# Moving GpSimd's scaling of k behind the weight residuals and the decayed q in a linear-attention recurrence

## The chip, the cores and the metric

The kernel runs on one NeuronCore of a Trainium2 chip. The metric is the device time of one execution in microseconds (us). The engines are TensorE (PE; its weight loads are shown as PEld), VectorE (DVE), ScalarE (ACT), GpSimd (POOL) and SyncE (SP, which issues DMAs). Each engine works through its own list in order and waits on semaphores.

## The reference

The input x (4 sequences of 1024 tokens, width 512) is normalised, and goes through a recurrent attention layer with 16 heads of width 128 and through a routed feed-forward layer; their product is added to x. What the change touches is the recurrence:

```python
q = silu(causal_dwconv(xn @ Wq, qconv_w, qconv_b))   # 4 taps
k = silu(causal_dwconv(xn @ Wk, kconv_w, kconv_b))
q = layernorm(q.reshape(Bs, Ls, H, DK), qn_w, qn_b)
k = layernorm(k.reshape(Bs, Ls, H, DK), kn_w, kn_b)
v = (xn @ Wv);  b = sigmoid(xn @ Wb + bb)
def step(S, inp):
    S = (1.0 - b) * S + b * (v_t[..., :, None] * k_t[..., None, :])
    o_t = jnp.einsum('bhvk,bhk->bhv', S, q_t)
```

The affine of a head's k is `k * kn_w + kn_b` behind the normalisation. The feed-forward layer keeps half of the tokens of each sequence by rank of a score.

## The kernel before

The kernel has four stages: the tokens (normalisation, gates, transposes), the recurrence, the feed-forward layer on the kept tokens, and the gated output. The change is in the recurrence, `stage_recurrence`. It treats 64 heads (4 sequences times 16), one head per step i, in a pipeline with lags: in step i the head A = i is projected and convolved, B = i-1 gets its silu, transpose and statistics, C = i-2 is transposed back and made ready, D = i-3 has its updates, scores, states and outputs computed. `nxt` = i+1 is the head whose weights are prepared. Two steps make a pair (par 0 and par 1); the par 1 step also ranks 128 tokens on VectorE, and GpSimd issues a small scatter behind it. Matrices in fp32 are multiplied as high and low parts: ScalarE writes `w_hi`, GpSimd writes the residual `w_lo = w_raw - w_hi`, and the same for `wv_hi`, `wv_lo`, which serve two heads and are made in par 0 steps.

The order of each engine in one step is written out by hand:

- TensorE: project q (L1020 to L1022); turn the normalised q of C, turn q of B (all turns are L999); first half of k's projection; turn k of C; second half; turn k of B; updates of D (L1079); scores of D (L1091); V projection (L1039 to L1041); outputs of D (L1105, L1107). The scores overwrite a half of PSUM from which ScalarE's `tokens(1)` reads: `after_step(pe, "k_tok", B_.i)`.
- ScalarE: silu of q of B (L787); ready(0) of C (L762); tap(0) of A (L772, the convolution's last tap); tokens(0) of B (L782); silu of k; `wv_hi` in par 0 (L803); `w_hi` (L808); ready(1) of C; tokens(1) of B (L782), which copies the turned k into `tok[1]`; tap(1); the normalisation of k in place in `tok[1]` (L821); the output copy of D (L827). tokens(1) has these waits:

```python
if j == 1:
    after_step(act, "k_weighted", B_.i - 1)
```

- VectorE: V times beta (L913); the decay scan of C (L924); ranks in par 1 (L970 to L983); three taps of q of A (L865); statistics of q and k of B (L873); variance (L886 to L894); states of D (L941, L945); scores of D times decays (L950); three taps of k of A (L865); k_state of C times decay (L958); shift (L899) and the normalisation of q (L903).
- GpSimd: `k_weighted` of C (L672, `tok[1]` times the norm's weight into `k_state`); `w_lo` of nxt (L679); `q_cum` of D (L686, q times the running decay); `wv_lo` in par 0 (L693); the add of the affine of C (L697, in place in `k_state`); the power function of B (L702, 1/sqrt of the variance).

TensorE's next step starts with a wait for the three taps of k (`k_conv`) and for `w_hi`, `w_lo`.

Of the kernel before, what the change touches and what calls it, by code (L numbers as in the profile page):

```python
# [7 lines left out]
ALU = mybir.AluOpType  # L8
ACT = mybir.ActivationFunctionType
F32 = mybir.dt.float32  # L10
# [35 lines left out]
def stand(eng, carrier):  # L46


    eng.sem_inc(carrier, 1)
# [414 lines left out]
def stage_recurrence(nc, s, a, scratch, keep, kept):  # L464
# [7 lines left out]
    with ExitStack() as ctx:  # L472
        def sb(name, shape, dt=F32):
            return ctx.enter_context(nc.sbuf_tensor("rc_" + name, shape, dt))

        def two(name, shape, dt=F32):
            return [sb(f"{name}{i}", shape, dt) for i in range(2)]

        def sem(name):
            return ctx.enter_context(nc.semaphore("rc_" + name))  # L480
# [3 lines left out]
        w_raw, w_hi, w_lo = keep["w_raw"], keep["w_hi"], keep["w_lo"]  # L484
        wv_raw, wv_hi, wv_lo = keep["wv_raw"], keep["wv_hi"], keep["wv_lo"]
# [5 lines left out]
        q_cm = two("q_cm", [P, L])  # L491
# [4 lines left out]
        cum_all = two("cum_all", [P, L])  # L496
        dmat = two("dmat", [P, NC, P])
        q_cum = sb("q_cum", [P, L])
# [28 lines left out]
        S = {n: sem(n) for n in names.split()}  # L527
# [6 lines left out]
        cum_loaded = [sem(f"cum_loaded{i}") for i in range(2)]  # L534
# [20 lines left out]
        def after_step(eng, name, i, per=1, part=None):  # L555

            if isinstance(i, int):
                if i < 0:
                    return
                i = min(i, N - 1)  # L560
            eng.wait_ge(S[name], per * i + (per if part is None else part))

        def after_pair(eng, semaphore, pair, per=16):

            if isinstance(pair, int) and pair < 0:
                return
            eng.wait_ge(semaphore, per * pair + per)
# [84 lines left out]
        @block.gpsimd  # L652
        def _(pool):
            nc.gpsimd.memset(minus_half[:], -0.5).then_inc(S["consts_set"], 1)
            for c in range(NC):
                last = nc.gpsimd.tensor_copy(chunk_ident[:, c], ident[:])
            last.then_inc(S["consts_set"], 1)
            nc.gpsimd.iota(token_row[:], pattern=[[1, L]], base=0, channel_multiplier=0,
                           allow_small_or_imprecise_dtypes=True).then_inc(S["consts_set"], 1)
            nc.gpsimd.iota(token_col[:], pattern=[[0, B], [P, NC]], base=0, channel_multiplier=1,  # L660
                           allow_small_or_imprecise_dtypes=True).then_inc(S["consts_set"], 1)
            nc.gpsimd.iota(first_slot[:], pattern=[[L, B], [0, NC]], base=0, channel_multiplier=0,
                           allow_small_or_imprecise_dtypes=True).then_inc(S["consts_set"], 1)

            def step(u, par):
                A_, B_, C_, D_, nxt = (At(u, par, lag) for lag in (0, LAG_B, LAG_C, LAG_D, -1))
                if C_.live:

                    k_tokens = k_state[C_.par]
                    after_step(pool, "k_normed", C_.i)  # L670
                    after_step(pool, "updates_mm", C_.i - 2)
                    nc.gpsimd.tensor_tensor(k_tokens[:], tok[1][:], k_norm_rows[:, 0:1].to_broadcast([P, NC, P]),  # L672
                                            ALU.mult).then_inc(S["k_weighted"], 1)
                if nxt.live:

                    after_step(pool, "w_hi_done", nxt.i)
                    after_step(pool, "k_projected", nxt.i - 2)
                    stand(pool, keep["carrier_pool"])
                    nc.gpsimd.tensor_tensor(w_lo[nxt.par][:], w_raw[nxt.par][:], w_hi[nxt.par][:].bitcast(F32),  # L679
                                            ALU.subtract).then_inc(S["w_lo_done"], 1)  # L680
                if D_.live:

                    after_step(pool, "q_ready", D_.i)
                    after_pair(pool, cum_loaded[D_.par], D_.pair)
                    after_step(pool, "outputs_mm", D_.i - 1)
                    nc.gpsimd.tensor_tensor(q_cum[:], q_cm[D_.par][:], cum_all[D_.par][:], ALU.mult  # L686
                                            ).then_inc(S["q_cum_done"], 1)
                if par == 0 and A_.live and not (isinstance(u, int) and u == 0):

                    after_step(pool, "wv_hi_done", u)  # L690
                    after_step(pool, "v_projected", A_.i - 1)
                    stand(pool, keep["carrier_pool"])
                    nc.gpsimd.tensor_tensor(wv_lo[:], wv_raw[:], wv_hi[:].bitcast(F32), ALU.subtract  # L693
                                            ).then_inc(S["wv_lo_done"], 1)
                if C_.live:
                    after_step(pool, "k_weighted", C_.i)
                    nc.gpsimd.tensor_tensor(k_state[C_.par][:], k_state[C_.par][:],  # L697
                                            k_norm_rows[:, 1:2].to_broadcast([P, NC, P]),
                                            ALU.add).then_inc(S["k_tokens_done"], 1)
                if B_.live:  # L700
                    after_step(pool, "small_done", B_.i, 6)
                    nc.gpsimd.tensor_tensor(small[:, 6], small[:, 5], minus_half[:], ALU.pow  # L702
                                            ).then_inc(S["rstd_done"], 1)

            pool.wait_ge(S["consts_loaded"], 16 * 7)

            def pair_steps(u):
                step(u, 0)
                step(u, 1)
                scatter(u)  # L710

            def scatter(u):

                pool.wait_ge(S["slot_done"], u + 1)
                pool.wait_ge(S["id_done"], u + 1)
                stand(pool, keep["carrier_pool"])
                nc.gpsimd.indirect_dma_start(
                    out=scratch["ids"], out_offset=bass.IndirectOffsetOnAxis(ap=slot[:, 0:1], axis=0),
                    in_=token_id[:, 0:1], in_offset=None).then_inc(S["scattered"], 16)

            for u in range(PEELED_PAIRS):
                pair_steps(u)
            with pool.Fori(PEELED_PAIRS, PAIRS - 2, 2) as u:
                pair_steps(u)
                pair_steps(u + 1)
            pair_steps(PAIRS - 2)
            pair_steps(PAIRS - 1)
            step(N // 2, N % 2)
            kept.gather(pool, 0)
            step((N + 1) // 2, (N + 1) % 2)  # L730
            kept.rstd_of(pool, 0)
            step((N + 2) // 2, (N + 2) % 2)
            pool.wait_ge(S["scattered"], 16 * PAIRS)
# [914 lines left out]
```

## Time and profile before

| | |
|---|---|
| median of 3 runs | 2820.19 us (2819.51 to 2823.3) |
| the profiled execution | 2817.73 us, span 2815.9 us |
| busy share of the span | PE 92%, PEld 81%, DVE 71%, ACT 42%, POOL 40% |
| the recurrence's steps | from about 147 to about 2010 us |
| mean granted clock of TensorE | 0.975 of 2.4 GHz |

Busy shares are averages over the four stages. A duration in a timeline is that of one group of instructions which follow one another, and the next may begin before it ends. In square brackets stands how long the engine was idle before the row, and what ended it. A granted clock of 1.00 is 2.4 GHz, 0.50 is 1.2 GHz.

### The profile page before, as it was taken

To read this page: it belongs to the slowest core of one execution; us is meant where nothing else is said; L and a number is where in the kernel's file an instruction comes from. 1 tells how busy PE (TensorE), PEld (TensorE's weight loads), DVE (VectorE), ACT (ScalarE), POOL (GpSimd) and SP (SyncE) were. 2 spreads that over 40 slices of the span, in tenths; PEclk is the share of its full clock that TensorE was granted. 3 is DMA by queue.
4 is the path that set the end of the run, shared out by engine and by line. 5 is a ranking of instruction groups with operands and counts; after the bars stand their busy time and mean duration, and the time that the engine had idled before them with its cause. 6 is when DMAs were issued, how large, how long until landed. Compare 5 with 4: busy or idle time off the path is not lost. (4 is left out here: it accounts for less than half of the span.)

```text
span 2815.9 us, 44455 instructions
## 1 busy us (share of the span) xinstructions
PE 2598.4 (92%) x15744; PEld 2287.7 (81%) x15744; DVE 2012.2 (71%) x3747; ACT 1178.2 (42%) x1585; POOL 1113.5 (40%) x515
## 2 busy tenths in 40 slices
PE   4799999999999989999999999999699999899997
PEld 4688888888888888888887888888678888788886
DVE  6688999889999889998998998899642121432332
ACT  5354454453544544545444445445352332322221
POOL 2156455455554554554554544645410000112121
PEclk9899999999999999999999999999899999999999
DMA  7222232532222342323324223322264110432220
GB/s 293 76 95 93 76 97 75 157 97 83 90 83 86 101 149 75 97 75 99 96 82 142 90 75 109 93 75 90 64 203 150 60 59 16 149 116 86 97 90 30
DMA packets 257476, 279.51 MB, mean 99 GB/s; under 512 B 55494, under 2 KB 211398, under 8 KB 252618
## 3 DMA queue, kind: packets, MB, share of 16 engines
q1 hardware_dynamic: 162506, 143.97, 16.4%
q10 hardware_dynamic: 86144, 109.06, 11.7%
q0 software_dynamic: 8704, 25.19, 2.9%
q8 instruction: 34, 0.56, 0.1%
q14 instruction: 88, 0.72, 0.1%
HBM read 214.70 MB, written 71.86 MB: 102 GB/s over the span
## 5 line engine op out<-in xcount | busy, mean ns | idle before, releaser
L865 DVE SCALAR_TENSOR_TENSOR xn_rows<-rc_ps_proj,rc_conv,xn_rows 128x1021 f32<-128x1021 f32 (+2 forms) x384 | 491.2, 1279 | 95.6 <-ACT xn_rows L772 86.5
L821 ACT ACTIVATE rc_tok_k<-rc_tok_k,rc_small 128x128 f32<-128x128 f32 x512 | 204.3, 482 | 819.3 <-DVE rc_small L899 819.3
L672 POOL TENSOR_TENSOR rc_k_state<-rc_tok_k,rc_k_norm_rows 128x1024 f32<-128x1024 f32 x64 | 247.6, 3868 | 529.0 <-ACT rc_tok_k L821 529.0
L1020 PE MATMUL rc_ps_proj<-xt_hi,w_hi 128*128 128x512 f32 x1024 | 418.5, 409 | 25.6 <-DMA xt_lo<-scratch_xt_lo 9.1
L1022 PE MATMUL rc_ps_proj<-xt_hi,w_lo 128*128 128x512 f32 x1024 | 403.8, 394 | 0.0
L1021 PE MATMUL rc_ps_proj<-xt_lo,w_hi 128*128 128x512 f32 x1024 | 402.9, 393 | 0.0
L1039 PE MATMUL rc_ps_proj<-wv_hi,xt_hi 128*128 128x256 f32 x1024 | 305.7, 299 | 62.5 <-POOL wv_lo L693 53.2
L1040 PE MATMUL rc_ps_proj<-wv_lo,xt_hi 128*128 128x256 f32 x1024 | 299.9, 293 | 0.0
L1041 PE MATMUL rc_ps_proj<-wv_hi,xt_lo 128*128 128x256 f32 x1024 | 299.5, 292 | 0.0
L679 POOL TENSOR_TENSOR w_lo<-w_raw,w_hi 128x1024 fp32r<-128x1024 f32 x63 | 150.7, 2391 | 326.4 <-ACT w_hi L808 326.4
L1039 PEld LDWEIGHTS rc_ps_proj<-wv_hi,xt_hi 128*128 128x128 f32 x1024 | 206.6, 202 | 68.8 <-issue 68.8
L1020 PEld LDWEIGHTS rc_ps_proj<-xt_hi,w_hi 128*128 128x128 f32 x1024 | 193.6, 189 | 71.1 <-issue 25.4
L1022 PEld LDWEIGHTS rc_ps_proj<-xt_hi,w_lo 128*128 128x128 f32 x1024 | 193.4, 189 | 42.4
L1021 PEld LDWEIGHTS rc_ps_proj<-xt_lo,w_hi 128*128 128x128 f32 x1024 | 193.8, 189 | 35.8
L1444 DVE TENSOR_TENSOR ff_wide_lo<-ff_wide,ff_wide_hi 128x512 fp32r<-128x512 f32 x64 | 44.3, 693 | 245.6 <-ACT ff_wide_hi L1359 245.5
L1105 PE MATMUL rc_ps_work<-rc_v_beta,rc_scores 128*128 128x128 f32 x1024 | 191.6, 279 | 21.5 <-DVE rc_scores L950 21.5
L702 POOL TENSOR_TENSOR rc_small<-rc_small,rc_minus_half 128x16 f32<-128x16 f32 x64 | 187.1, 2924 | 55.3 <-DVE rc_small L894 55.3
L1040 PEld LDWEIGHTS rc_ps_proj<-wv_lo,xt_hi 128*128 128x128 f32 x1024 | 207.0, 202 | 0.0
L1041 PEld LDWEIGHTS rc_ps_proj<-wv_hi,xt_lo 128*128 128x128 f32 x1024 | 206.9, 202 | 0.0
L1440 DVE TENSOR_TENSOR gt_wide<-gt_ps_turn,gt_gate 128x512 f32<-128x512 f32 x64 | 44.2, 691 | 194.3 <-ACT gt_gate L1352 194.3
L1107 PE MATMUL rc_ps_work<-rc_states,rc_q_cum 128*128 128x128 f32 x896 | 175.6, 278 | 0.0
L1105 PEld LDWEIGHTS rc_ps_work<-rc_v_beta,rc_scores 128*128 128x128 f32 x1024 | 152.9, 195 | 25.1 <-issue 25.1
(170 smaller groups left out, 6179.3 us busy)
## 6 DMA issues: line engine op xcount, KB each, us to landing
rc_decay_all<-scratch_decay ACTq DMA_DIRECT2D x64, 512.0 KB, 3.7
rc_cum_all<-scratch_cum ACTq DMA_DIRECT2D x64, 512.0 KB, 3.6
scratch_o<-rc_o_sb ACTq DMA_DIRECT2D x64, 512.0 KB, 3.4
w_raw<-in_wq SPq DMA_DIRECT2D x64, 256.0 KB, 3.4
w_raw<-in_wk SPq DMA_DIRECT2D x64, 256.0 KB, 3.7
wv_raw<-in_wv SPq DMA_DIRECT2D x32, 512.0 KB, 3.4
rc_score_all<-scratch_score SPq DMA_DIRECT2D x32, 512.0 KB, 4.2
raw<-in_w SPq DMA_DIRECT2D x16, 512.0 KB, 4.4
```

The lines of the kernel that those rows point to most:

```text
L672: nc.gpsimd.tensor_tensor(k_tokens[:], tok[1][:], k_norm_rows[:, 0:1].to_broadcast([P, NC, P]), ALU.mult).then_inc(S["k_weighted"], 1)
L702: nc.gpsimd.tensor_tensor(small[:, 6], small[:, 5], minus_half[:], ALU.pow).then_inc(S["rstd_done"], 1)
L821: last = nc.scalar.activation(tok[1][:, c], tok[1][:, c], ACT.Identity, bias=small[:, 7, 1, c:c + 1], scale=small[:, 6, 1, c:c + 1])
L865: nc.vector.scalar_tensor_tensor(out=act_cm[j][:, back:], in0=projected[:, 0:L - back], scalar=conv[par][:, j, t:t + 1], in1=act_cm[j][:, ...
L1020: nc.tensor.matmul(out, hi, xt_hi[:, k, cols], start=k == 0, stop=False)
L1021: nc.tensor.matmul(out, hi, xt_lo[:, k, cols], start=False, stop=False)
L1022: last = nc.tensor.matmul(out, lo, xt_hi[:, k, cols], start=False, stop=k == KC - 1)
L1039: nc.tensor.matmul(out, xt_hi[:, k, cols], wv_hi[:, k], start=k == 0, stop=False)
L1040: nc.tensor.matmul(out, xt_hi[:, k, cols], wv_lo[:, k], start=False, stop=False)
L1041: last = nc.tensor.matmul(out, xt_lo[:, k, cols], wv_hi[:, k], start=False, stop=k == KC - 1)
L1105: last = nc.tensor.matmul(out, scores[:, c], values, start=True, stop=c == 0)
L1107: last = nc.tensor.matmul(out, q_cum[:, c * P:(c + 1) * P], states[:, c - 1], start=False, stop=True)
```

## The change

In each step, GpSimd's list is put in another order. The instructions, their waits and the buffers stay as they are. Before: `k_weighted`, `w_lo`, `q_cum`, `wv_lo` (par 0), affine add, power function. After: `w_lo`, `wv_lo` (par 0), `q_cum`, `k_weighted`, affine add, power function.

```diff
             def step(u, par):
                 A_, B_, C_, D_, nxt = (At(u, par, lag) for lag in (0, LAG_B, LAG_C, LAG_D, -1))
+                if nxt.live:
+                    after_step(pool, "w_hi_done", nxt.i)
+                    after_step(pool, "k_projected", nxt.i - 2)
+                    stand(pool, keep["carrier_pool"])
+                    nc.gpsimd.tensor_tensor(w_lo[nxt.par][:], w_raw[nxt.par][:], w_hi[nxt.par][:].bitcast(F32),
+                                            ALU.subtract).then_inc(S["w_lo_done"], 1)
+                if par == 0 and A_.live and not (isinstance(u, int) and u == 0):
+                    after_step(pool, "wv_hi_done", u)
+                    after_step(pool, "v_projected", A_.i - 1)
+                    ...
+                if D_.live:
+                    after_step(pool, "q_ready", D_.i)
+                    after_pair(pool, cum_loaded[D_.par], D_.pair)
+                    after_step(pool, "outputs_mm", D_.i - 1)
+                    nc.gpsimd.tensor_tensor(q_cum[:], q_cm[D_.par][:], cum_all[D_.par][:], ALU.mult
+                                            ).then_inc(S["q_cum_done"], 1)
                 if C_.live:
                     k_tokens = k_state[C_.par]
                     ...
                     nc.gpsimd.tensor_tensor(k_tokens[:], tok[1][:], k_norm_rows[:, 0:1].to_broadcast([P, NC, P]),
                                             ALU.mult).then_inc(S["k_weighted"], 1)
-                if nxt.live:
-                    (w_lo as above)
-                if D_.live:
-                    (q_cum as above)
-                if par == 0 and A_.live and not (isinstance(u, int) and u == 0):
-                    (wv_lo as above)
                 if C_.live:
                     after_step(pool, "k_weighted", C_.i)
```

## Rows read from the trace of the kernel before

**Rows 1.** The waits of the whole span: total us, times, longest us.

```profile
...
POOL rc_k_state L672 <- ACT rc_tok_k L821: 529.0, 63, 9.2
...
PE rc_ps_proj L1039 <- POOL wv_lo L693: 53.2, 28, 2.2
...
```

**Rows 2.** TensorE's timeline over one pair: start us, length us, line, tiles, [idle before it].

```profile
...
1063.06 0.49 PE L1020 MATMUL rc_ps_proj<-xt_hi,w_hi 128*128 128x512 f32 x1 [0.38 <-DVE xn_rows L865]
...
1069.98 1.09 PE L999 MATMUL rc_ps_work<-ident,xn_rows 128*128 128x128 f32 x8 [0.31 <-ACT xn_rows L787]
...
1079.76 1.95 PE L1091 MATMUL rc_ps_work<-rc_q_cm,rc_k_cm 128*128 128x128 f32 x16
...
1087.30 0.60 PE L1105 MATMUL rc_ps_work<-rc_v_beta,rc_scores 128*128 128x128 f32 x4
...
1107.67 1.95 PE L1091 MATMUL rc_ps_work<-rc_q_cm,rc_k_cm 128*128 128x128 f32 x16
1111.49 0.38 PE L1039 MATMUL rc_ps_proj<-wv_hi,xt_hi 128*128 128x256 f32 x1 [1.87 <-POOL wv_lo L693]
...
1118.83 0.60 PE L1105 MATMUL rc_ps_work<-rc_v_beta,rc_scores 128*128 128x128 f32 x4
...
1122.09 0.48 PE L1020 MATMUL rc_ps_proj<-xt_hi,w_hi 128*128 128x512 f32 x1
...
```

**Rows 3.** VectorE's timeline over the same pair.

```profile
...
1058.86 3.91 DVE L865 SCALAR_TENSOR_TENSOR xn_rows<-rc_ps_proj,rc_conv,xn_rows 128x1021 f32<-128x1021 f32 x3
...
1079.46 1.65 DVE L873 BATCH_NORM_STATS2 rc_stats<-rc_tok_k 128x6 f32<-128x128 f32 x8
...
1086.75 3.91 DVE L865 SCALAR_TENSOR_TENSOR xn_rows<-rc_ps_proj,rc_conv,xn_rows 128x1021 f32<-128x1021 f32 x3
...
1111.22 2.42 DVE L887 TENSOR_TENSOR rc_small<-rc_stats 128x16 f32<-128x16 f32 x1
...
```

**Rows 4.** GpSimd's timeline over the same pair.

```profile
...
1067.35 4.33 POOL L672 TENSOR_TENSOR rc_k_state<-rc_tok_k,rc_k_norm_rows 128x1024 f32<-128x1024 f32 x1 [9.22 <-ACT rc_tok_k L821]
1075.46 2.40 POOL L679 TENSOR_TENSOR w_lo<-w_raw,w_hi 128x1024 fp32r<-128x1024 f32 x1 [3.78 <-ACT w_hi L808]
...
1080.13 2.38 POOL L697 TENSOR_TENSOR rc_k_state<-rc_k_state,rc_k_norm_rows 128x1024 f32<-128x1024 f32 x1
...
1108.91 2.34 POOL L693 TENSOR_TENSOR wv_lo<-wv_raw,wv_hi 128x1024 fp32r<-128x1024 f32 x1
1111.21 2.38 POOL L697 TENSOR_TENSOR rc_k_state<-rc_k_state,rc_k_norm_rows 128x1024 f32<-128x1024 f32 x1
...
```

**Rows 5.** ScalarE's timeline over the same pair.

```profile
...
1071.19 1.21 ACT L772 ACTIVATE xn_rows<-rc_ps_proj,rc_conv 128x1024 f32<-128x1024 f32 x1 [0.17 <-PE rc_ps_work L999]
...
1074.15 1.05 ACT L808 ACTIVATE w_hi<-w_raw 128x1024 fp32r<-128x1024 f32 x1
...
1078.40 1.02 ACT L782 ACTIVATE rc_tok_k<-rc_ps_work 128x1024 f32<-128x1024 f32 x1 [2.10 <-PE rc_ps_work L999]
...
1099.09 1.21 ACT L772 ACTIVATE xn_rows<-rc_ps_proj,rc_conv 128x1024 f32<-128x1024 f32 x1
...
1102.99 1.05 ACT L808 ACTIVATE w_hi<-w_raw 128x1024 fp32r<-128x1024 f32 x1
...
```

**Rows 6.** Line 672 on GpSimd, k_weighted: duration ns, least, median, most.

```profile
...
L672 POOL TENSOR_TENSOR rc_k_state<-rc_tok_k,rc_k_norm_rows x64: 2341/4301/4333, 147.1 to 2009.5; 128x1024 f32<-128x1024 f32 x64
...
```

**Rows 7.** Line 886 on VectorE, first instruction of the variance: duration ns.

```profile
...
L886 DVE TENSOR_TENSOR rc_small<-rc_stats x64: 186/1442/2415, 139.0 to 1998.7; 128x16 f32<-128x16 f32 x64
...
```

**Rows 8.** TensorE's timeline late in the recurrence, output matmuls after a wait.

```profile
...
2003.30 0.70 PE L1105 MATMUL rc_ps_work<-rc_v_beta,rc_scores 128*128 128x128 f32 x4 [3.69 <-DVE rc_scores L950]
...
```

**Rows 9.** Windows: length, busy us of PE, PEld, DVE, ACT, POOL; clock; DMA; GB/s.

```profile
...
161.00:164.00 3.00, 2.43 (x11) 2.46 (x12) 2.96 (x7) 0.00 (x0) 2.80 (x2) 0.50 0.95 271
164.00:167.00 3.00, 3.00 (x16) 3.00 (x15) 2.90 (x6) 0.00 (x0) 2.46 (x1) 0.50 0.17 57
...
1113.00:1116.30 3.30, 3.30 (x18) 3.30 (x17) 3.07 (x11) 0.00 (x0) 2.65 (x2) 0.50 0.33 116
...
```

More of the change, by code:

```diff
@@ L666, in step @@
                 A_, B_, C_, D_, nxt = (At(u, par, lag) for lag in (0, LAG_B, LAG_C, LAG_D, -1))
+                if nxt.live:
[7 more added lines that the diff above has]
+                    after_step(pool, "v_projected", A_.i - 1)
+                    stand(pool, keep["carrier_pool"])
+                    nc.gpsimd.tensor_tensor(wv_lo[:], wv_raw[:], wv_hi[:].bitcast(F32), ALU.subtract
+                                            ).then_inc(S["wv_lo_done"], 1)
+                if D_.live:
[4 more added lines that the diff above has]
+                                            ).then_inc(S["q_cum_done"], 1)
                 if C_.live:
@@ L673, in step @@
                                             ALU.mult).then_inc(S["k_weighted"], 1)
-                if nxt.live:
[L676 to L680, printed above, removed]
-                if D_.live:
[L683 to L687, printed above, removed]
-                if par == 0 and A_.live and not (isinstance(u, int) and u == 0):
[L690 to L694, printed above, removed]
                 if C_.live:
```

## The prediction

> **What bounds the kernel now.** The chain that ended last was of no use here: it lies wholly in the last stage, and the change is in the recurrence. So I read the waits first, then the timelines of the four engines over one pair of steps (a step of even number, "even", which also splits the V weights, and a step of odd number, "odd", which also does the ranks), and last the granted clock. The waits show GpSimd early in one place and late in another: it stands 529.0 us before the affine of k, waiting for ScalarE's normalised k, and TensorE waits for GpSimd's wv_lo 28 times, 53.2 us in all [rows 1]. The first tells that GpSimd does the scaling of k (k_weighted) in time that is otherwise idle. One pair lasts from TensorE's start at 1063.06 to its start at 1122.09, 59.03 us [rows 2]. TensorE is nearly always busy, and a step starts when two things are there: its own last output matmuls, and VectorE's three taps of the k convolution, which end at 1062.77, only 0.29 us before TensorE starts [rows 2, 3]. So VectorE and TensorE bound the step together, and GpSimd bounds neither, but for the 1.87 us ahead of the V projection in even steps [rows 2]. Anything put into the path of these two lengthens the step.
>
> **The change, part by part.** No instruction is added or removed; GpSimd's in-order list is turned round. k_weighted, which now starts at 1067.35 as soon as k is normalised, goes behind w_lo, wv_lo and q_cum [rows 4]. All that follows is what this does to the readers of each.
>
> *k_weighted.* It reads tok_k, and ScalarE's tokens(1) writes the next head's k into that same buffer, so it waits for k_weighted. Now k_weighted is long done when tokens(1) starts (1078.40, held by TensorE's turn alone) [rows 5]. After, GpSimd's first instruction is w_lo, which waits for ScalarE's w_hi (ends 1074.15+1.05 = 1075.20 in the odd step, 1102.99+1.05 = 1104.04 in the even one) [rows 5]. k_weighted then takes the very place that the affine's add has now: it starts at 1080.13 and at 1111.21 [rows 4]. Its price: now 4.33 us at 1067.35, and over all 64 between 2.341 and 4.333 [rows 6]; the add of the same 128x1024 takes 2.38 [rows 4]. I take 2.35, the low end, because at its new place VectorE runs only the q convolution and q statistics, beside which w_lo keeps 2.40 [rows 4]; the high end stays as a rival. So k_weighted ends (call it K) at 1082.48 and 1113.56, which is 7.28 and 9.52 us after w_hi ends. With 0.2 us from engine to engine (GpSimd's wv_lo ends at 1111.25, TensorE starts at 1111.49 [rows 2, 4]), tokens(1) is held until 1082.7 instead of 1078.40 in the odd step, 4.3 us, and until 1113.8 in the even one.
>
> *Who is queued behind tokens(1).* On ScalarE: tap(1) of k, then the normalisation of k and the output copy. On VectorE: the statistics of k wait for it, and behind them stand variance, states, scores and the k convolution. On TensorE: the score matmuls L1091 wait for it, because they overwrite the PSUM half that tokens(1) reads, and behind them stand the V projection, the outputs and the next step. Both of the two paths that bound the step are hit.
>
> *TensorE's path.* K + 0.2, tokens(1) 1.02 [rows 5], 0.05, then L1091 to the first L1105 7.54 (1079.76 to 1087.30), and outputs to the next start 3.26 (1118.83 to 1122.09) [rows 2]: the next step starts at K+12.07. From a start to ScalarE's tap(0) it is now 8.13 us (1063.06 to 1071.19 [rows 2, 5]), of which 0.31 to 0.33 is TensorE waiting for silu before its turn of q (1069.98 [rows 2]), a wait that goes when TensorE is the late one: 7.80. From tap(0) to the end of w_hi 4.01 (1071.19 to 1075.20) and 4.95 (1099.09 to 1104.04) [rows 5]. The cycle closes: odd 7.80+4.01+7.28+12.07 = 31.16 us, even 7.80+4.95+9.52+12.07 = 34.34 us, together 65.50.
>
> *VectorE's path.* From the statistics of k to the end of the k convolution 11.20 us (1079.46 to 1090.66) [rows 3], of which about 1.25 is L886, 1.44 at the median where it takes 0.19 at the least [rows 7]; that wait goes, since it lasts until GpSimd's add ends (1082.51 [rows 4]) and the add now ends before L886 is reached. So the convolution ends at K+0.2+1.02+0.1+9.95 = K+11.27. From there to tap(0) 8.42 (1062.77 to 1071.19 [rows 3, 5]). Odd 8.42+4.01+7.28+11.27 = 30.98, even 34.16: 0.2 us under TensorE's, which therefore decides.
>
> *What it costs.* 65.50-59.03 = 6.47 us a pair. The new order bites where both the scaling of k and w_lo are live: steps 2 to 62, 61 steps, 30.5 pairs: 197 us.
>
> *The clock.* TensorE now stands idle between the update matmuls L1079 and L1091, from 1079.76 to K+1.27 = 1083.75, 4.0 us in odd steps, and 7.2 us in even ones, from 1107.67 to 1114.83 [rows 2]. What an idle stretch does is seen already: after the 1.87 us ahead of 1111.49 the granted clock was 0.50 (1.2 of 2.4 GHz) from 1113.0 to 1116.3, and after 3.69 us of idleness before 2003.30 the output matmuls took 0.70 and more where those at 1118.83 take 0.60 [rows 2, 8, 9]. Now this costs nothing, since the wait for VectorE takes it up. After, it lies on TensorE's path, in L1091 and the V projection. A stretch of 3.3 us at half pace costs at most 1.65 us; I take 1.5. The bounds: nothing, if the fall comes inside the idleness, and twice that, since the stretch from 161 to 167 was at 0.50 throughout [rows 9]. 61 x 1.5 = 92 us.
>
> The Trainium skill, "TensorE: Matmul & The Clock Gate", section "HAM oscillation — how this bites in real kernels", says that a loop which idles TensorE in every pass makes its clock fall again in every pass. The trace so far agrees, with 0.50 behind the gap at 1111.49 [rows 2, 9]; by the rule the sum has the 92 us, without it it ends at 197.
>
> *The rest costs nothing.* w_lo keeps its place, so the weight loads on SP, which wait for it, do too. wv_lo comes 2.34 us sooner, but its reader, the V projection, now stands behind L1091 and is later than that: the 1.87 us are swallowed, not gained. q_cum comes 2.34 us later in even steps, ending at 1111.2; its readers are the outputs, from 1118.83 on [rows 2, 4]. The add comes right after K, at K+2.4; its reader is after the k convolution, at K+11.3. The power function waits for the variance (K+3.8), ends near K+7, and is read near K+12; in odd steps the scatter, the one DMA that GpSimd issues there, follows it as now. If the power function took 5 us more, it would start to count.
>
> Sum: 2817.7 (the profiled execution; the median of the runs is 2.5 above it, and I set the sum between) + 197 + 92 = 3107 to 3109: **3108 us**, +10.2%.
>
> **The rivals.**
> - *Clock loss off the path.* The drop falls wholly within the idle time, above all the 7.2 us of even steps. Against it: the drop at 1113.0 came 1.5 us after work had begun [rows 2, 9]. 2819+197 = 3016. Chance 0.13.
> - *Clock loss twice as large.* As from 161 to 167, 6 us at half pace after one gap [rows 9]: 3.0 us a step, 183 in all: 3199. Chance 0.10.
> - *k_weighted still takes 4.33.* It would have to wait at its new place for something of VectorE's; 1.95 x 61 = 119 us more: 3227. Against it: w_lo and the add run there at 2.40 and 2.38 [rows 4]. Chance 0.04.
> - *Faster.* The waits of VectorE beside GpSimd go (L887 stands 2.42 us until GpSimd's add ends at 1113.6, L886 1.44 at the median [rows 3, 7]) and so does the 1.87 us gap, and tokens(1) is not held. The gain is about 1.9 us per even step, 31 x 1.9 = 59: 2760. It decides if K comes before 1078.2; it is reckoned at 1082.48, 4.3 us behind that point, so something would have to make w_hi that much sooner. Chance 0.03. The Trainium skill, "SBUF — State Buffer", section "Who interferes with whom", has the rule behind this rival: GpSimd and a VectorE instruction with two SBUF inputs lock one another out for a whole instruction. The trace agrees where L887 ends with GpSimd's add [rows 3, 4].
> - *Nothing changes.* tokens(1) does not in fact wait for k_weighted behind the three. Only if the order of the list did not hold on the engine; 2820. Chance 0.02.
>
> **How the numbers follow.** The forecast, with a clock cost between 1 and 2 us a step and the path terms within 0.5 us of a step, has 0.68 and its own range 3060 to 3160. The range of 3010 to 3180 takes in the case without clock loss and leaves out the doubled one, the slow k_weighted and the two small ones. A difference of 0.2%, 5.6 us, is about what a measurement of this kernel can tell from none. Faster 0.03, same 0.02, slower 0.95.
>
> **What would show it.** Right: ScalarE's tokens(1) waits for GpSimd's k_weighted in 61 steps, some 3 to 7 us each; k_weighted at 2.35 us with no idle time ahead of it; a gap of some 4 and 7 us on TensorE ahead of L1091 (its line there), with granted clock 0.5 behind it in each step; L886 and L887 near 0.2 us; a pair of 68.5 us. Wrong: a clock of 1.00 behind the gaps, or k_weighted at 4.3 us, or a pair of 59. The forecast falls if ScalarE's w_hi is reached sooner than I reckon, since all of K hangs on it, or if VectorE has a wait of its own that I take for work.

## The result and the profile after

The changed kernel takes 3152.8 us (median of 4 runs, 3145.0 to 3159.4), the kernel before 2821.1 us: a ratio of 1.117 (95% interval 1.115 to 1.120), or 332 us more. The forecast was 3108, or 288 more, in a range of 3010 to 3180. The execution profiled is the longest of the four, 3159.4 us, 341.6 us longer in span than the one of before.

The page of the changed kernel, first its span and the busy time of three engines:

```profile
span 3157.5 us, 44469 instructions
...
PE 2696.9 (85%) x15744; PEld 2404.2 (76%) x15744; DVE 1817.0 (58%) x3747; ACT 1177.0 (37%) x1585; POOL 1012.9 (32%) x515
...
```

VectorE and GpSimd are busy 195 and 101 us less than before, though their work is the same: most of the instructions that stood while the other engine ran no longer do. That is what the change saves; it puts more idle time in. The waits of the whole span (total us, times, longest):

```profile
...
POOL w_lo L672 <- ACT w_hi L808: 1230.1, 63, 27.3
...
ACT rc_tok_k L782 <- POOL rc_k_state L693: 449.1, 61, 8.5
DVE rc_stats L873 <- ACT rc_tok_k L782: 447.5, 63, 8.9
...
PE rc_ps_work L1091 <- ACT rc_tok_k L782: 335.9, 60, 7.3
...
```

The second line is the wait that the prediction named, and it occurs 61 times. TensorE waits before the scores (L1091) because tokens(1) is late; the third line is the same lateness on VectorE's path. GpSimd's timeline over one pair (L672 is now w_lo, L693 k_weighted, L697 the add), beside [rows 4]:

```profile
...
1110.53 2.40 POOL L672 TENSOR_TENSOR w_lo<-w_raw,w_hi 128x1024 fp32r<-128x1024 f32 x1 [20.29 <-ACT w_hi L808]
...
1115.19 2.34 POOL L693 TENSOR_TENSOR rc_k_state<-rc_tok_k,rc_k_norm_rows 128x1024 f32<-128x1024 f32 x1
...
1144.09 2.36 POOL L672 TENSOR_TENSOR w_lo<-w_raw,w_hi 128x1024 fp32r<-128x1024 f32 x1 [18.69 <-ACT w_hi L808]
...
1151.01 2.33 POOL L693 TENSOR_TENSOR rc_k_state<-rc_tok_k,rc_k_norm_rows 128x1024 f32<-128x1024 f32 x1
1153.42 2.35 POOL L697 TENSOR_TENSOR rc_k_state<-rc_k_state,rc_k_norm_rows 128x1024 f32<-128x1024 f32 x1
...
```

k_weighted ends (K) at 1117.53 and 1153.34, 7.26 and 9.46 us after w_hi (ScalarE's rows, below); 7.28 and 9.52 were reckoned. It takes 2.34 us, not 4.3. Why it took 4.33 before is in VectorE's timeline of before, beside [rows 4]:

```profile
...
1067.22 2.28 DVE L924 TENSOR_TENSOR_SCAN rc_dmat<-rc_decay_all,rc_chunk_ident 128x1024 f32<-128x1024 f32 x1
...
```

The decay scan, with two inputs in SBUF, starts 0.13 us ahead of k_weighted and ends at 1069.50; k_weighted ends 2.18 us after that. In 50 of the 64 steps the scan starts first, and k_weighted takes 4.2 to 4.33 us; in the other 14 it does not, and k_weighted takes 2.34 to 2.38. ScalarE's timeline, beside [rows 5]:

```profile
...
1109.21 1.06 ACT L808 ACTIVATE w_hi<-w_raw 128x1024 fp32r<-128x1024 f32 x1
...
1117.65 1.02 ACT L782 ACTIVATE rc_tok_k<-rc_ps_work 128x1024 f32<-128x1024 f32 x1 [6.27 <-POOL rc_k_state L693]
...
1142.82 1.06 ACT L808 ACTIVATE w_hi<-w_raw 128x1024 fp32r<-128x1024 f32 x1
...
1153.46 1.02 ACT L782 ACTIVATE rc_tok_k<-rc_ps_work 128x1024 f32<-128x1024 f32 x1 [8.49 <-POOL rc_k_state L693]
...
```

TensorE's timeline over the same pair, beside [rows 2]:

```profile
...
1098.53 0.48 PE L1020 MATMUL rc_ps_proj<-xt_hi,w_hi 128*128 128x512 f32 x1
...
1118.81 3.38 PE L1091 MATMUL rc_ps_work<-rc_q_cm,rc_k_cm 128*128 128x128 f32 x16 [3.95 <-ACT rc_tok_k L782]
...
1127.78 0.60 PE L1105 MATMUL rc_ps_work<-rc_v_beta,rc_scores 128*128 128x128 f32 x4
...
1131.05 0.48 PE L1020 MATMUL rc_ps_proj<-xt_hi,w_hi 128*128 128x512 f32 x1
...
1154.63 3.75 PE L1091 MATMUL rc_ps_work<-rc_q_cm,rc_k_cm 128*128 128x128 f32 x16 [7.26 <-ACT rc_tok_k L782]
...
1167.64 0.48 PE L1020 MATMUL rc_ps_proj<-xt_hi,w_hi 128*128 128x512 f32 x1
...
```

The odd step lasts from 1098.53 to 1131.05, 32.52 us, and the even one to 1167.64, 36.59 us, 69.11 together, against 68.5 in the prediction. From start to K they take 19.00 and 22.29 us, where 19.09 and 22.27 were reckoned. What is longer than reckoned lies behind K: 13.52 and 14.30 us to the next start, not 12.07. L1091 takes 3.38 and 3.75 us where it took 1.95. The windows (length, busy us of PE, PEld, DVE, ACT, POOL, then granted clock) say why:

```profile
...
170.00:2330.00 2160.00, 1803.84 (x11499) 1659.18 (x11498) 1457.29 (x3173) 853.65 (x1136) 855.12 (x368) 0.90 0.26 79
...
1118.80:1122.20 3.40, 3.39 (x18) 3.40 (x19) 3.23 (x17) 0.96 (x1) 2.10 (x2) 0.58 0.00 0
...
1154.60:1158.00 3.40, 3.37 (x16) 3.40 (x17) 3.24 (x17) 0.98 (x1) 2.09 (x2) 0.50 0.00 0
...
```

Behind the gaps of 3.95 and 7.26 us the clock is at 0.58 and 0.50. Over the steps it is 0.90, where it was 0.98. L1091 takes 3.35 us or more behind all but three of the 60 waits (2.63 to 2.74 there), so the clock falls in practically every step. In the kernel before, the gap of 1.9 us ahead of the V projection had a low clock behind it in 13 of 30 even steps: the projection took 7.5 us in these and 6.0 in the others. VectorE's variance, all 64 steps, beside [rows 7]:

```profile
...
L886 DVE TENSOR_TENSOR rc_small<-rc_stats 128x16 f32<-128x16 f32 x64 | 12.0, 187 | 2.2
L887 DVE TENSOR_TENSOR rc_small<-rc_stats 128x16 f32<-128x16 f32 x64 | 11.5, 179 | 0.0
...
```

L886 now takes 187 ns on average: the wait beside GpSimd is gone. What it buys is less than what VectorE now waits before the statistics of k (447.5 us in the waits above, 50.8 before the change).

### The profile page after: what moved, and what is told of

The parts are those of the page before. It is cut to its first block and busy times, and to the rows that moved or that the text cites. A ratio compares the mean times of both kernels' runs of the same rounds, so it can differ in the third digit from the quotient of the medians.

```text
span 3157.5 us, 44469 instructions
## 1 busy us (share of the span) xinstructions
PE 2696.9 (85%) x15744; PEld 2404.2 (76%) x15744; DVE 1817.0 (58%) x3747; ACT 1177.0 (37%) x1585; POOL 1012.9 (32%) x515
## 5 line engine op out<-in xcount | busy, mean ns | idle before, releaser
L672 POOL TENSOR_TENSOR w_lo<-w_raw,w_hi 128x1024 fp32r<-128x1024 f32 x63 | 150.0, 2381 | 1230.1 <-ACT w_hi L808 1230.1
L1091 PE MATMUL rc_ps_work<-rc_q_cm,rc_k_cm 128*128 128x128 f32 x1024 | 226.0, 410 | 335.9 <-ACT rc_tok_k L782 335.9
L1091 PEld LDWEIGHTS rc_ps_work<-rc_q_cm,rc_k_cm 128*128 128x128 f32 x1024 | 211.4, 315 | 345.6 <-issue 345.6
L873 DVE BATCH_NORM_STATS2 rc_stats<-rc_tok_k 128x6 f32<-128x128 f32 x512 | 105.4, 279 | 447.5 <-ACT rc_tok_k L782 447.5
L1039 PE MATMUL rc_ps_proj<-wv_hi,xt_hi 128*128 128x256 f32 x1024 | 317.8, 310 | 5.7 <-issue 2.9
L1040 PE MATMUL rc_ps_proj<-wv_lo,xt_hi 128*128 128x256 f32 x1024 | 308.5, 301 | 0.0
L1041 PE MATMUL rc_ps_proj<-wv_hi,xt_lo 128*128 128x256 f32 x1024 | 306.0, 299 | 0.0
L782 ACT ACTIVATE rc_tok_k<-rc_ps_work 128x1024 f32<-128x1024 f32 x64 | 65.5, 1023 | 453.8 <-POOL rc_k_state L693 449.1
L1039 PEld LDWEIGHTS rc_ps_proj<-wv_hi,xt_hi 128*128 128x128 f32 x1024 | 219.7, 215 | 6.3 <-issue 6.3
L1040 PEld LDWEIGHTS rc_ps_proj<-wv_lo,xt_hi 128*128 128x128 f32 x1024 | 217.1, 212 | 0.0
L1041 PEld LDWEIGHTS rc_ps_proj<-wv_hi,xt_lo 128*128 128x128 f32 x1024 | 215.7, 211 | 0.0
```

The lines of the kernel that those rows point to most:

```text
L1039: nc.tensor.matmul(out, xt_hi[:, k, cols], wv_hi[:, k], start=k == 0, stop=False)
L1040: nc.tensor.matmul(out, xt_hi[:, k, cols], wv_lo[:, k], start=False, stop=False)
L1041: last = nc.tensor.matmul(out, xt_lo[:, k, cols], wv_hi[:, k], start=False, stop=k == KC - 1)
L1091: last = nc.tensor.matmul(work(par, SC)[:, t], k_cm[D_.par][:, t], q_cm[D_.par][:, t], start=True, stop=True)
```

## The experiments

Besides the time of a kernel, the length of each step is given, read from ScalarE's timeline as the distance from one normalisation of k to the next (that is VectorE's pace: it starts with VectorE's shift). Before the change it is 27.9 us in odd and 31.1 to 31.5 in even steps, after it on average 33.4 and 36.6 (three steps in which a new sequence is loaded left out; together they are 11 us longer than the other even steps before the change, and 15 after it). "The hold" is the wait of tokens(1) for k_weighted. "A lock" is an instruction of VectorE that stands until one of GpSimd's ends, or the other way round.

**Where k_weighted stands (`e1_k_second`).** Behind w_lo alone (the list is given as an order, - is the changed kernel):

```diff
-    w_lo, wv_lo, q_cum, k_weighted, add, power
+    w_lo, k_weighted, wv_lo, q_cum, add, power
```

> Order of GpSimd: w_lo, k_weighted, wv_lo, q_cum, add, power. Theory (the hold of tokens(1) plus the locks of VectorE beside GpSimd): k_weighted ends 4.9 us after w_hi in every step, so tokens(1) is held only 2.0 us in odd and 2.8 us in even steps and TensorE's cycle alone would be 28.8 and about 31.2 us; but q_cum (even: wv_lo and q_cum) and the add now run while VectorE does the variance, whose first instructions stand until the add ends, 2.35 us later than before the change in each step. Pair about 59.0+4.7 = 63.7 us, 2820+145 = 2965 us (2930 to 3020, the clock adding what is on the path). Rival, the hold alone and no locks: odd steps 1 us longer, even ones as before, 2850 us.

Measured: 2962.4 us, 1.0496 (1.0476 to 1.0517). Steps 30.2 and 33.4 to 33.8 us, 63.7 a pair on average, as expected. The hold alone was reckoned at 2850, so most of this comes from the locks. GpSimd and VectorE in one even step:

```profile
...
1130.32 2.35 POOL L693 TENSOR_TENSOR rc_q_cum<-rc_q_cm,rc_cum_all 128x1024 f32<-128x1024 f32 x1
1132.64 2.40 POOL L697 TENSOR_TENSOR rc_k_state<-rc_k_state,rc_k_norm_rows 128x1024 f32<-128x1024 f32 x1
...
```

```profile
...
1130.91 1.81 DVE L886 TENSOR_TENSOR rc_small<-rc_stats 128x16 f32<-128x16 f32 x1
1132.64 2.43 DVE L887 TENSOR_TENSOR rc_small<-rc_stats 128x16 f32<-128x16 f32 x1
1135.00 0.17 DVE L888 TENSOR_TENSOR rc_small<-rc_stats 128x16 f32<-128x16 f32 x1
...
```

L886 ends when q_cum ends (1132.67) and L887 when the add ends (1135.04); L888 is then free and takes 0.17 us.

**wv_lo ahead of q_cum (`e2_wv_before_q`).** The other half of the change alone, with k_weighted first (- is the kernel before):

```diff
-    k_weighted, w_lo, q_cum, wv_lo, add, power
+    k_weighted, w_lo, wv_lo, q_cum, add, power
```

> Order of GpSimd: k_weighted first as before, then w_lo, wv_lo, q_cum, add, power: only wv_lo and q_cum are swapped. Theory: TensorE's 1.87 us ahead of the V projection go, but VectorE's variance still stands until the add ends, so the gap only moves to the outputs' wait for the scores: 2821 us within 0.3%. Rival, the gap is on the path: 31 x 1.87 = 58 us less, 2763 us.

Measured: 2837.8 us, 1.0053 (1.0035 to 1.0071), outside of the 0.3% that was written. The rival is out. Most of the 17 us are in the odd steps, 27.9 to 28.5 us, now and then 29.8. The gap has moved, and grown:

```profile
...
1073.53 1.19 PE L1105 MATMUL rc_ps_work<-rc_v_beta,rc_scores 128*128 128x128 f32 x4 [2.90 <-DVE rc_scores L950]
...
```

TensorE waits 2.90 us before the outputs of this even step, the first matmuls after it take 1.19 us in place of 0.60, and the next, odd, step starts late. That the clock makes the 17 us agrees with this, but no run separates it.

**No hold (`e3_two_tok_k`).** The changed order, with two buffers for the normalised k; to make room, `token_row` lies in a tile of a later stage:

```diff
-    after_step(act, "k_weighted", B_.i - 1)
-    nc.scalar.activation(tok[j][:], ...)
+    after_step(act, "k_weighted", B_.i - 2)
+    nc.scalar.activation((tok_q, tok_k[B_.par])[j][:], ...)
```

> The changed order, but the normalised k has two buffers, so that tokens(1) no longer waits for the k_weighted of the same step. Theory: the hold of some 6 and 8 us a step goes, and with it TensorE's gaps ahead of the scores and their low clock; what is left is that k_weighted and the add now run while VectorE does the variance, whose instructions stand until the add ends, 2.35 us later than before the change: 2820+145 = 2965 us (2900 to 3000). Rival 1, the hold is everything: 2821 us or, with wv_lo sooner, down to 2763. Rival 2, the cost of the change lies elsewhere (w_hi, DMA): it stays near 3150.

Measured: 2986.1 us, 1.0582 (1.0562 to 1.0603): half of the cost goes, half stays. Steps 31.1 and 33.7 us. ScalarE's tokens(1) waits for TensorE's turn alone, as before the change:

```profile
...
1130.48 1.02 ACT L783 ACTIVATE rc_tok_k<-rc_ps_work 128x1024 f32<-128x1024 f32 x1 [0.88 <-PE rc_ps_work L1000]
...
```

But VectorE's variance stands beside GpSimd, instruction after instruction, L888, L889 and L895 here:

```profile
...
1133.38 2.43 DVE L888 TENSOR_TENSOR rc_small<-rc_stats 128x16 f32<-128x16 f32 x1
1135.73 2.44 DVE L889 TENSOR_TENSOR rc_small<-rc_stats 128x16 f32<-128x16 f32 x1
...
1138.42 2.23 DVE L895 SCALAR_TENSOR_TENSOR rc_small<-rc_small 128x16 f32<-128x16 f32 x1
...
```

```profile
...
1133.37 2.40 POOL L687 TENSOR_TENSOR rc_q_cum<-rc_q_cm,rc_cum_all 128x1024 f32<-128x1024 f32 x1
1135.71 2.42 POOL L694 TENSOR_TENSOR rc_k_state<-rc_tok_k,rc_k_norm_rows 128x1024 f32<-128x1024 f32 x1
1138.21 2.41 POOL L698 TENSOR_TENSOR rc_k_state<-rc_k_state,rc_k_norm_rows 128x1024 f32<-128x1024 f32 x1
...
```

They end at 1135.81, 1138.17 and 1140.65, just where GpSimd's q_cum, k_weighted and add end (1135.77, 1138.13, 1140.62). TensorE then waits 4.76 us for the scores:

```profile
...
1144.43 1.19 PE L1106 MATMUL rc_ps_work<-rc_v_beta,rc_scores 128*128 128x128 f32 x4 [4.76 <-DVE rc_scores L951]
...
```

The expected 2965 left out that a third instruction would be caught, and the clock behind this gap. So the late place of k_weighted has two costs, of which only one shows at a time: it holds tokens(1), and with the hold gone it locks VectorE. That moving `token_row` costs nothing was not tested by itself.

**The gap filled (`e4_filled`, `e7_filled_wide`).** The changed kernel with matmuls of no use in TensorE's gap, whose results the V projection overwrites:

```diff
                     last.then_inc(S["updates_mm"], 1)
+                    if A_.live:
+                        after_step(pe, "q_conv", A_.i, PAD)
+                        for _ in range((52, 26)[par]):
+                            nc.tensor.matmul(ps_proj[:, par, 0:2 * P], xt_hi[:, 0, BANK:BANK + P],
+                                             xt_hi[:, 0, BANK:BANK + 2 * P], start=True, stop=True)
```

> The changed kernel, with 26 (odd steps) or 52 (even steps) matmuls of 256 columns of no use on TensorE in its gap ahead of the scores, into a PSUM half that the V projection overwrites later; they take some 3.1 and 6.2 us of gaps of 3.95 and 7.26 us. They keep the granted clock up and hold nothing. Theory: the measured 332 us are 197 us of path and 135 us of clock (2.2 us a step, not 1.5): 3018 us, granted clock 0.97 or more. Rival, the path terms were too small and the clock is what was forecast (92 us): 3060 us. Rival, the clock costs nothing here: 3153.

> The changed kernel with the gap on TensorE filled by half as many matmuls of twice the columns (13 and 27 of 512). In the narrow filling the steps took 31.1 and 34.7 us but every fourth, at the turn of the loop, up to 4 us more, with TensorE idle for no wait that the profile shows; I take that for the loop's longer body (78 more matmuls a pair). Theory: with half of them it shrinks, 3067 falls to 3020 to 3045, with steps of 31.1 and 34.7 us elsewhere. Rival, it has nothing to do with the number of instructions: 3067.

Measured: 3066.8 us (1.0873, 1.0851 to 1.0896) and 3065.8 us (1.0866, 1.0848 to 1.0884), granted clock 0.979 in both. TensorE in one odd step of the first, and, after the second "...", at the next start:

```profile
...
1133.78 3.35 PE L1085 MATMUL rc_ps_proj<-xt_hi 128*128 128x256 f32 x26
1138.06 2.02 PE L1096 MATMUL rc_ps_work<-rc_q_cm,rc_k_cm 128*128 128x128 f32 x16 [0.92 <-ACT rc_tok_k L782]
...
1153.14 0.79 PE L1020 MATMUL rc_ps_proj<-xt_hi,w_hi 128*128 128x512 f32 x1 [3.96 <-issue]
...
```

```profile
...
170.00:2240.00 2070.00, 1967.53 (x13878) 1818.12 (x13876) 1453.52 (x3165) 857.77 (x1139) 863.24 (x368) 0.99 0.28 84
...
```

Away from the turn of the loop the steps are 31.1 and 34.7 us, against 31.2 and 34.3 reckoned without any clock loss: the path terms were right within 0.4 us, and some 2 us a step of the changed kernel are the clock, as the first expectation had it.

The time is not down to 3018 because of idle time like that of the row at 1153.14: at the turn of the loop, every fourth step, TensorE stands for nothing that the waits show, 13 times, 32.4 us in all. It is 1.8 to 2.2 us ten times, and 4.0 to 4.4 us three times, where a new sequence is loaded as well. In 8 of the 13 passes matmuls behind it run at half pace (0.63 us in place of 0.39). Half as many and wider matmuls do not change that (35.7 us in all), so the guess that the number of extra matmuls sets the size of it fell. But the two kernels do differ from the changed one in how instructions are loaded. The DMA queue of 16 KB instruction packets, first in the page of the changed kernel, then in that of `e4_filled`:

```profile
...
q8 instruction: 34, 0.56, 0.1%
...
```

```profile
...
q8 instruction: 167, 2.74, 0.4%
...
```

From 400 to 1800 us this queue brings no packet in the kernels before and after, 102 in `e4_filled` and 92 in `e7_filled_wide`, and one of them ends inside the 3.96 us ahead of 1153.14 (at 1151.25). That points to a loop body which no longer stays loaded from one pass to the next, and for which the 80 added matmuls a pass of `e7_filled_wide` are enough; no run separates it.

**The change in even steps alone (`e10_even_only`).** Odd steps have the order from before.

> The change in even steps alone (w_lo, wv_lo, q_cum, k_weighted, add), odd steps in the order from before. Theory: the even step costs what it costs in the changed kernel, 36.0 to 37.1 us against 31.1 to 31.5, of which 3.4 are the path and some 2 the clock, odd steps stay at 27.9: 31 x 5.3 = 164 us more, 2985 us (2960 to 3000). Rival, the clock comes only when every step has a gap: 31 x 3.4 = 105, 2926 us.

Measured: 2990.6 us, 1.0596 (1.0571 to 1.0620), within the expected. But the steps are 34.1 to 34.5 (even) and 30.1 to 30.6 (odd), not 36 and 27.9. The even step shows VectorE's path as reckoned, 34.16. VectorE's convolution of k (L893 here) and TensorE's next start (L1048) at the end of one even step:

```profile
...
1016.31 3.91 DVE L893 SCALAR_TENSOR_TENSOR xn_rows<-rc_ps_proj,rc_conv,xn_rows 128x1021 f32<-128x1021 f32 x3
...
```

```profile
...
1023.46 0.48 PE L1048 MATMUL rc_ps_proj<-xt_hi,w_hi 128*128 128x512 f32 x1
...
```

VectorE is done at 1020.22, TensorE starts 3.24 us later, where it was 0.29 before the change. So TensorE, which alone has the clock's share, ends the even step late and passes that on to VectorE in the odd step. That fits the two lengths, but was not tested by itself. My expectation of the single steps was wrong; that their sum came out is luck in so far as the surplus moved from one step to the other.

**Better orders.** In the kernel before, the add runs beside the variance, and wv_lo too in even steps. Three orders move the add away, the last of them q_cum too (`e5_add_early`, `e8_v_first`, `e6_both_early`):

```diff
-    k_weighted, w_lo, q_cum, wv_lo, add, power
+    k_weighted, add, w_lo, wv_lo, q_cum, power      (e5)
+    k_weighted, add, wv_lo, w_lo, q_cum, power      (e8)
+    k_weighted, q_cum, add, w_lo, wv_lo, power      (e6)
```

> Order of GpSimd: k_weighted and the add first, then w_lo, wv_lo, q_cum, power. k_weighted holds nobody, and the add no longer runs beside VectorE's variance. Theory (locks beside GpSimd are what bounds the kernel before): in even steps only wv_lo and q_cum are left there, the variance is free 2.4 us sooner, and with wv_lo sooner TensorE's 1.87 us go too, so an even step falls from 31.1 to about 29.3 us; in odd steps the variance is 1.25 us sooner but the ranks stand about 1.6 us behind the add, 27.9 stays. 31 x 1.8 = 56 us less: 2765 us. Rival: the add beside the ranks costs odd steps 2 us or more: 2800 to 2830.

> Order of GpSimd: k_weighted, the add, wv_lo, w_lo, q_cum, power. As the run with the add alone early, but wv_lo starts 0.9 us sooner, as soon as wv_hi is there, so that all three residual and decay products end 0.9 us sooner in even steps. Theory: if VectorE bounds the even step, up to 0.9 us less than there (2740), if TensorE does, the same (2765). Rival: w_lo, now later by 1.4 us in even steps, holds the weight loads and the next step: slower than there.

> Order of GpSimd: k_weighted, q_cum and the add first, then w_lo, wv_lo, power. Theory: even steps as in the run with the add alone early or slightly better, 29.2 us; in odd steps two instructions of GpSimd now run beside the ranks, and VectorE's two-input instructions of the ranks stand until each ends, 2 to 4 us more than now, less 1.25: 28.5 to 30.5. 2770 to 2850 us. Rival, locks do not matter there: 2765 us or less.

| | us | ratio, 95% interval | odd, even steps |
|---|---|---|---|
| e5 | 2818.4 | 0.9988 (0.9979 to 0.9997) | 30.5, 28.9 to 29.3 |
| e8 | 2788.3 | 0.9880 (0.9865 to 0.9895) | 30.5, 27.9 to 28.4 |
| e6 | 2756.7 | 0.9761 (0.9748 to 0.9774) | 30.4, 26.8 to 27.2 |

Even steps gain 2.2 (e5), 3.1 (e8) and 4.3 us (e6). Odd steps lose 2.6 in all three, the rival of the first of them: the add runs beside the ranks. The three steps with a new sequence are no longer than the other even ones here, which gives another 11 us; with it the steps add up to the times of the table within 7 us. e5's expected 2765 failed by the odd steps, and e8's 2740 or 2765 for the same reason; against e5 its even steps are 0.9 to 1.0 us shorter, as its first branch had it. e6 ends below its expected range because its even steps take 27, not 29.2 us; its rival's number came close, but not its reason, for the locks do matter in odd steps. VectorE in an odd step of e5 (L976 and L981 read two SBUF tiles; L886 is free):

```profile
...
1011.74 3.20 DVE L976 SCALAR_TENSOR_TENSOR rc_equal<-rc_token_row,rc_token_col,rc_equal 128x1024 f32<-128x1024 f32 x1
...
1015.07 2.18 DVE L981 SCALAR_TENSOR_TENSOR rc_slot<-rc_greater,rc_ties,rc_first_slot 128x1 int32<-128x1 f32 x1
...
1024.34 0.19 DVE L886 TENSOR_TENSOR rc_small<-rc_stats 128x16 f32<-128x16 f32 x1
...
```

and all ranks of e6 (count, busy us, mean ns):

```profile
...
L976 DVE SCALAR_TENSOR_TENSOR rc_equal<-rc_token_row,rc_token_col,rc_equal 128x1024 f32<-128x1024 f32 x32 | 101.1, 3159 | 3.9
...
L981 DVE SCALAR_TENSOR_TENSOR rc_slot<-rc_greater,rc_ties,rc_first_slot 128x1 int32<-128x1 f32 x32 | 67.0, 2095 | 3.6
...
L886 DVE TENSOR_TENSOR rc_small<-rc_stats 128x16 f32<-128x16 f32 x64 | 12.0, 188 | 2.2
...
```

L976 took 1348 ns and L981 282 ns on average before the change. q_cum ahead of the add costs nothing more in odd steps, since e6's are no longer than e5's. The last run uses both findings (`e9_by_parity`), e6's order in even steps and the old order in odd ones:

> Two orders: in even steps k_weighted, q_cum, add, w_lo, wv_lo, power (an even step measured 26.8 to 27.2 us with that order); in odd steps, which have the ranks, the order from before the change (27.9 us, where the early add cost 30.5). Theory: the cost of an order lies in its own step, by what VectorE does beside it, so a pair is 26.9+27.9 = 54.8 us against 59.1: 31 x 4.3 = 133 us less, 2688 us (2675 to 2710). Rival, the gain of the even steps hangs on TensorE and VectorE having slack from a slow odd step: 2720 to 2760.

Measured: 2702.4 us, 0.9581 (0.9562 to 0.9600), the fastest here, and within the expected. Steps 28.2 and 26.8 to 27.2 us. The shown instructions of the ranks and, in the even step, the variance are free. What still stands is the odd step's L914 (the line of L886), and the comparison at the head of the ranks, with 1.5 us as before:

```profile
...
1012.92 1.28 DVE L1004 SCALAR_TENSOR_TENSOR rc_equal<-rc_token_row,rc_token_col,rc_equal 128x1024 f32<-128x1024 f32 x1
...
1014.34 0.22 DVE L1009 SCALAR_TENSOR_TENSOR rc_slot<-rc_greater,rc_ties,rc_first_slot 128x1 int32<-128x1 f32 x1
...
1021.91 1.55 DVE L914 TENSOR_TENSOR rc_small<-rc_stats 128x16 f32<-128x16 f32 x1
...
1049.95 0.19 DVE L914 TENSOR_TENSOR rc_small<-rc_stats 128x16 f32<-128x16 f32 x1
...
```

## Why the prediction was right

- *The hold.* 61 waits of tokens(1) for k_weighted, as said. They are 6.27 and 8.49 us in the pair shown and 7.4 on average, not "some 3 to 7": that line of the prediction measured from the former start of tokens(1), though ScalarE, with nothing else to do, is there sooner. K is what counts for the path, and it was right. e3 removes the hold and with it 167 of 332 us, and locks of VectorE take the place of the other half. Right.
- *K and the path.* Start to K within 0.1 us; steps of 31.1 and 34.7 us in e4 against 31.16 and 34.34, which makes 204 us where 197 were reckoned. They stand.
- *The price of k_weighted*, 2.34 us. Right; the rival of 4.33 is out, because the decay scan of VectorE beside which it took that long is over by then. (Its surplus is 1.98 us a step, 121 us, not 1.95 and 119.)
- *The clock.* The mechanism was right, the size was not: this is the term that makes 3108 into 3153. "A stretch of 3.3 us at half pace costs at most 1.65 us; I take 1.5" was read from one stretch behind a gap of 1.87 us. Behind the longer gaps the cost is 13.52-12.07 = 1.45 us in the odd and 14.30-12.07 = 2.23 us in the even step of this pair, whose odd step is one of the shortest; over all steps it is 33.4-31.2 = 2.2 and 36.6-34.3 = 2.3. 61 x 2.25 = 137 us, and 197+137 = 334 for 332 measured. That this closes is no check by itself, since the 2.25 are what the steps had over the path; the check is e4, in which the odd steps fall by 2.3 and the even ones away from the turn of the loop to 34.7. The miss of 45 us lies inside the range, whose width came from this term.
- *The locks go.* L886 and L887 at 0.19 and 0.18 us, as said. The rival "faster" had the right mechanism but the wrong order for it: e6 and e9 are that rival with tokens(1) not held, and they gain 66 and 120 us. It was priced at 59, as if an even step could lose no more than TensorE's gap of 1.87 us; with e9 it loses 4.3.
- *The rest costs nothing.* wv_lo's wait before the V projection is gone from the list of waits. Only the three steps with a new sequence cost 4 us more than before, which the sum did not have.

## What to carry to other kernels

Before an instruction is moved down an in-order list, look at who overwrites what it reads: the cost of this change is a buffer that is free some 7 us too late, not the work. Where GpSimd and VectorE hold one another up, as here, GpSimd's list is chosen by what VectorE does at that moment, and the best list may differ between steps of different content (0.958 here, with nothing but order). Where TensorE gets a new gap in every step, add to the path the clock behind it, priced from gaps of that length.

## What was not expected of the hardware

- A VectorE instruction of 16 columns can take 2.4 us beside GpSimd, one after another, each until one GpSimd instruction ends (L888, L889, L895 in e3). The instructions that stood had two inputs in SBUF, and so did L981, of one column. One with a single input did too, the comparison L974: 1490 ns on average before, where k_weighted ends some 0.96 us after it has begun, and 753 after the change, when GpSimd is idle at that moment. The convolution taps, with one input in PSUM, and the statistics did not.
- It goes the other way too: GpSimd's k_weighted took 4.33 us where VectorE's decay scan had begun 0.13 us before it, and 2.34 to 2.38 where the scan had not begun.
- Keeping TensorE busy with matmuls whose results nobody reads gave back 86 of the 332 us.
- TensorE stood some 2 us at the turn of the loop in ten of its passes in the filled kernels, and 4 us and more in three. Instruction packets arrive all through the loop in these kernels and not in the others; that this is the cause is likely, but not shown.
